# A 512-wide layer in plain float32 instead of three products of high and low fp32r parts

## The reference

```python
# layer 0
h = relu(x)
h = depthwise 3x3 conv of h, dilation 2, + dw_bias
h = h @ pw + pw_bias                      # 256 -> 256
x = h * inv + (beta - moving_mean * inv)  # inv = gamma * rsqrt(moving_var + eps)
# layer 1: a scan over all 56*56 positions on a spiral from the centre outwards
def step(g, (ci, ni, nm, nc)):
    local = g[:, ci, :]
    neigh = (g[:, ni, :] * nm).sum(axis=1) / nc      # up to 4 neighbours
    u = concatenate([local, neigh])                  # 512
    y = tanh(u @ w1 + b1) @ w2 + b2                  # 512 -> 512 -> 1
    g[:, ci, :] = local + y * w_y
```

## Time and profile before

| | |
|---|---|
| median of 3 runs | 5248.01 us (5244.97 to 5255.16) |
| span of the profiled execution | 5242.1 us |
| TensorE / its weight loads busy | 4812.6 us (92%) / 4082.9 us (78%) |
| VectorE busy | 4437.0 us (85%) |
| ScalarE / GpSimd busy | 2045.2 us (39%) / 1133.7 us (22%) |
| mean granted TensorE clock | 0.973 of full speed |
| HBM traffic | 128 GB/s over the span |

### The profile page before, as it was taken

How to read it: one execution, slowest core, us unless ns; L and a number is a source line. 1 busy time by engine, 2 the same in 40 slices (tenths; PEclk the granted TensorE clock), 3 DMA queues, 4 the chain that set the end, 5 groups by cost and what they waited for, 6 DMA issues and landing times.

```text
span 5242.1 us, 101723 instructions
## 1 busy us (share of the span) xinstructions
PE 4812.6 (92%) x26981; PEld 4082.9 (78%) x26981; DVE 4437.0 (85%) x7868; ACT 2045.2 (39%) x3253; POOL 1133.7 (22%) x1806
## 2 busy tenths in 40 slices
PE   4888888988888887999999999999999999999998
PEld 3777777887777776888888877788877887888776
DVE  6999999999999994777777877778777887888888
ACT  3555555555555552333333333333333333333332
POOL 1000000000000000333333333333333333333332
PEclk8999999999999998999999999999999999999999
DMA  4454544544444443433334333333333333333332
GB/s 104 159 164 153 163 154 155 169 163 154 152 159 148 156 151 150 118 114 112 115 109 114 116 111 111 109 110 115 108 105 104 112 109 104 107 112 104 106 100 72
DMA packets 253378, 661.81 MB, mean 126 GB/s; under 512 B 82210, under 2 KB 83234, under 8 KB 238370
## 3 DMA queue, kind: packets, MB, share of 16 engines
q1 hardware_dynamic: 209778, 552.76, 34.6%
q0 software_dynamic: 43056, 102.88, 6.1%
HBM read 347.00 MB, written 323.09 MB: 128 GB/s over the span
## 4 chain that ended last, share of the span: by engine, by line
PE 53%; issue 28%; DVE 17%; DVEq 1%; DMA 1%; SPq 0%; ACT 0%; POOL 0%; ACTq 0%; POOLq 0%
PE psum L785 13%; PE psum L783 13%; PE psum L784 13%; DVE dw_rows L568 9%; PE psum L771 6%; PE psum L779 3%; DVE bias_tmp L617 2%; DVE u_lo L602 2%; PE psum L744 2%; PE psum L750 2%; DVE relu_rows L638 1%; DVE gn_out L625 1%; DVE gn_out L610 0%; DVE win_tmp L643 0%; PE psum L728 0%
## 5 line engine op out<-in xcount | busy, mean ns | idle before, releaser
L568 DVE SCALAR_TENSOR_TENSOR dw_rows<-relu_rows,taps,dw_rows 128x896 f32<-128x896 f32 x1744 | 1863.0, 1145 | 104.0 <-ACT dw_rows L416 46.6
L783 PE MATMUL psum<-w_hi,u_hi 128*128 128x512 f32 x3588 | 1583.8, 441 | 0.0
L785 PE MATMUL psum<-w_hi,u_lo 128*128 128x512 f32 x3588 | 1413.6, 394 | 0.0
L468 ACT ACTIVATE gn_out<-gn_out 128x512 f32<-128x512 f32 x897 | 567.1, 632 | 2147.6 <-DVE gn_out L610 1840.4
L784 PE MATMUL psum<-w_lo,u_hi 128*128 128x512 f32 x3588 | 1401.5, 391 | 0.0
L377 POOL DMA_INDIRECT out<-gn_out,idx_col x897 | 881.9, 983 | 2034.7 <-POOLq L383 1375.4
L610 DVE SCALAR_TENSOR_TENSOR gn_out<-v_row,s_col,psum 128x512 f32<-128x512 f32 x897 | 668.7, 746 | 456.3 <-PE psum L785 387.0
L744 PE MATMUL psum<-pw,dw_rows 128*128 128x256 f32 x3136 | 846.1, 394 | 0.0
L750 PE MATMUL psum<-ident,dw_rows 128*128 128x128 f32 x6216 | 836.5, 279 | 0.0
L750 PEld LDWEIGHTS psum<-ident,dw_rows 128*128 128x128 f32 x6216 | 757.7, 145 | 87.2 <-issue 8.2
L785 PEld LDWEIGHTS psum<-w_hi,u_lo 128*128 128x128 f32 x3588 | 676.5, 189 | 155.4
(11 more groups left out here) (75 smaller groups left out, 2728.3 us busy)
## 6 DMA issues: line engine op xcount, KB each, us to landing
gn_out<-scratch SPq DMA_DIRECT2D x3588, 64.0 KB
scratch<-gn_out SPq DMA_DIRECT2D x112, 1792.0 KB, 5.7
x_tok<-x SPq DMA_DIRECT2D x112, 896.0 KB, 6.6
out<-gn_out,idx_col POOLq DMA_INDIRECT x897
relu_rows<-coef SPq DMA_DIRECT2D x1, 5830.5 KB
gn_out<-L_conv_w SPq DMA_DIRECT2D x2, 512.0 KB, 7.6
store_idx<-store_row SPq DMA_DIRECT2D x1, 448.5 KB, 7.7
w_row<-L_conv_w SPq DMA_DIRECT2D x1, 256.0 KB, 6.0
```

Of the source, the lines that this page charges most:

```text
L468: act.activation(th[:, cc % 2, :], pre_s[:, cc % 2, :], ACT.Tanh).then_inc(th_ready, 1)
L568: ins = dve.scalar_tensor_tensor(out=dst, in0=src, scalar=w, in1=dst, op0=ALU.mult, op1=ALU.add)
L783: pe.matmul(bank, hi, w1_hi[:, k, :], start=False, stop=False)
L785: last = pe.matmul(bank, lo, w1_hi[:, k, :], start=False, stop=k == 2 * CK - 1)
```

## The change

The high and low parts go. `w1_sb` holds the folded w1 and `u_sb` the transposed u, both float32, and `hidden` has one matmul per block of 128 instead of three. `low_part` on VectorE is gone with its semaphore; ScalarE's copy (now `copy_u`) counts up `u_copied`, which TensorE waits for in both places. The four starting credits are given by ScalarE. In the setup four subtractions on VectorE go.

```diff
-        w1_hi = sb("w1_hi", [P, 2 * CK, HID], f32r)
-        w1_lo = sb("w1_lo", [P, 2 * CK, HID], f32r)
-        u_hi = sb("u_hi", [P, U_SLOTS, 2 * C], f32r)
-        u_lo = sb("u_lo", [P, U_SLOTS, 2 * C], f32r)
+        w1_sb = sb("w1_sb", [P, 2 * CK, HID])
+        u_sb = sb("u_sb", [P, U_SLOTS, 2 * C])
...
+            act.sem_inc(u_copied, 4)
...
-            def high_part(c, cc):
+            def copy_u(c, cc):
                 act.wait_ge(u_ready, c + 1)
                 act.wait_ge(pre_ready, c + 1)
-                act.activation(u_hi[:, cc % U_SLOTS, :], psum[:, cc % 4, :], ACT.Copy).then_inc(hi_ready, 1)
+                act.activation(u_sb[:, cc % U_SLOTS, :], psum[:, cc % 4, :], ACT.Copy).then_inc(u_copied, 1)
...
-                link(dve.tensor_copy(w1_hi[:, k, :], w))
-                link(dve.tensor_tensor(w1_lo[:, k, :], w, w1_hi[:, k, :].bitcast(f32), ALU.subtract))
+                link(dve.tensor_copy(w1_sb[:, k, :], w))
...
-            def low_part(c, cc):
-
-                dve.wait_ge(hi_ready, c + 1)
-                slot = cc % U_SLOTS
-                dve.tensor_tensor(u_lo[:, slot, :], psum[:, cc % 4, :], u_hi[:, slot, :].bitcast(f32),
-                                  ALU.subtract).then_inc(lo_ready, 1)
...
-                if not isinstance(c, int) or c + AHEAD < TILES:
-                    low_part(c + AHEAD, cc + AHEAD)
...
-                pe.wait_ge(lo_ready, c + 1)
+                pe.wait_ge(u_copied, c + 1)
...
-                pe.wait_ge(lo_ready, 4 + c + 1)
+                pe.wait_ge(u_copied, 4 + c + 1)
                 pe.wait_ge(pres_ready, c + 1)
                 bank = psum[:, 4 + cc % 4, :]
                 pe.matmul(bank, pick[:, :], bias_rows[:, C:C + HID], start=True, stop=False)
                 for k in range(2 * CK):
-                    hi = u_hi[:, cc % U_SLOTS, P * k:P * (k + 1)]
-                    lo = u_lo[:, cc % U_SLOTS, P * k:P * (k + 1)]
-                    pe.matmul(bank, hi, w1_hi[:, k, :], start=False, stop=False)
-                    pe.matmul(bank, hi, w1_lo[:, k, :], start=False, stop=False)
-                    last = pe.matmul(bank, lo, w1_hi[:, k, :], start=False, stop=k == 2 * CK - 1)
+                    last = pe.matmul(bank, u_sb[:, cc % U_SLOTS, P * k:P * (k + 1)], w1_sb[:, k, :],
+                                     start=False, stop=k == 2 * CK - 1)
                 last.then_inc(pre_ready, 1)
```

More of the change, by code:

```diff
@@ L126, in build @@
           load_row, store_row, coef, wrap, side, scratch, out):
-    f32, f32r = mybir.dt.float32, mybir.dt.float32r
+    f32 = mybir.dt.float32
     bf16, i32 = mybir.dt.bfloat16, mybir.dt.int32
@@ L226, in build @@
         u_ready = sem("u_ready")
-        hi_ready = sem("hi_ready")
-        lo_ready = sem("lo_ready")
+        u_copied = sem("u_copied")
         pre_ready = sem("pre_ready")
@@ L456, in _ @@
             row_steps(act, step, ROWS - 1 + OUT_LAG)
-            def high_part(c, cc):
+            def copy_u(c, cc):
                 act.wait_ge(u_ready, c + 1)
                 act.wait_ge(pre_ready, c + 1)
-                act.activation(u_hi[:, cc % U_SLOTS, :], psum[:, cc % 4, :], ACT.Copy).then_inc(hi_ready, 1)
+                act.activation(u_sb[:, cc % U_SLOTS, :], psum[:, cc % 4, :], ACT.Copy).then_inc(u_copied, 1)
             def tile(c, cc, *_):
                 if not isinstance(c, int) or c + AHEAD < TILES:
-                    high_part(c + AHEAD, cc + AHEAD)
+                    copy_u(c + AHEAD, cc + AHEAD)
                 act.wait_ge(pres_ready, 4 + c + 1)
@@ L470, in _ @@
             for c in range(AHEAD):
-                high_part(c, c)
+                copy_u(c, c)
             tile(0, 0)
@@ L541, in _ @@
             dve.sem_inc(s_ready, 1)
-            dve.sem_inc(lo_ready, 4)
             dve.sem_inc(out_ready, TILE_SLOTS)
@@ L661, in y_of @@
                 return y_lvl[:, level % 2, g:g + 1]
-            for c in range(AHEAD):
-                low_part(c, c)
             centre_y = y_of(1, 0)
             add_s(0, 0, 0, 0)
-            low_part(AHEAD, AHEAD)
             dot(0, 0, centre_y)
@@ L802 @@
 SETUP_T = SETUP_CST + 4
-SETUP_V = SETUP_T + 4 * CK + 1 + 2 + (1 + 6) + (1 + 3) + 1
+SETUP_V = SETUP_T + 2 * CK + 1 + 2 + (1 + 6) + (1 + 3) + 1
 CONV_TAPS = [(1, 0), (1, 2)] + [(ky, kx) for ky in (0, 2) for kx in range(3)]
```

## The result

The changed kernel takes 5765.8 us in the median of 4 runs (5762.2 to 5767.6), the kernel before 5247.4 us. The ratio is 1.098 (95% interval 1.097 to 1.100): 518 us slower. The profiled execution took 5765.57 us, with a span of 5763.8 us.

What follows compares the result with a forecast made beforehand. TensorE was taken to set the second phase's pace, 3.40 us a tile. Span 5242.1 + 512.4 (products) + 20 (jumps) - 2.9 (setup) = 5771.6 us, plus 5.9 around the span: 5777 us, range 5745 to 5825.

Steps and rivals of the forecast that it cites:

- Products: Second phase: twelve fp32r matmuls become eight float32 records of 0.4286 us; tile 3.40 to 4.08 us, +512.4 us.
- Subtraction: VectorE loses 0.683 us per tile, 612 us in all: worth nothing as work; ScalarE's copy gets about 6.5 us to spare.
- Jumps and wrap levels: Second phase's loop jumps: most of 96.9 us excess swallowed, 20 us of TensorE's own idle time stays; bounds 0 and 70.
- Last stage: Last 32 tiles, one per level: VectorE's chain shrinks from 3.98 to 3.78 us, so TensorE's 4.08 us sets the pace.
- ScalarE: Its copy of u writes float32 instead of fp32r, still 0.58 us, its wait stays hidden: no change in time.
- Setup: Before the first phase, four VectorE subtractions of 0.69 us go, about 0.72 us each with the gap: -2.9 us.
- First phase: The phase before the changed lines is untouched: 0 us.
- Around the span: The median of the runs lies 5.9 us over the profiled span (5248.0 against 5242.1), so 5.9 us was added.
- stalls stay: Rival: at loop jumps 6.5 us to spare is not enough, or TensorE idles 3 us; up to 70 us, 5827; chance 0.12.
- every pass costs as much as an fp32r product: Rival: each of a float32 record's two passes takes 0.229 us, 0.236 us more a tile, 5988 us; chance 0.04.
- the late copy: Rival: ScalarE's copy of u comes late every time, tile longer than 4.08 us, some 5900 us; chance 0.02.
- faster: Rival: a float32 record starts every 0.229 us, TensorE's tile 2.48 us, VectorE's chain binds some stages; about 4435 us; chance 0.02.

Runs made afterwards that it cites:

- the bf16 rows: The kernel before with its high and low parts in bf16 instead of fp32r, same twelve products: 5150.5 us, ratio 0.982.
- two versions with pieces: The changed kernel with each 512-column float32 matmul cut into two pieces (8 matmuls a tile) or three (12): 5803.0 us and 5855.3 us.
- the run with two products: The changed kernel with two fp32r products per block (u by w1's high and low parts) instead of one float32 product: 4568.0 us, ratio 0.870.

## Why the prediction was right, point by point

- *Products.* Right, and the whole result hangs on it. A record starts every 0.43 us, a tile takes 4.085 us against my 4.08. From the first to the last tile it is 518.6 us more (3661.9 - 3143.3), where I had 512.4 + 20; 4.5 us of that is the third digit of the pace (3660.2 against 3655.7). The Trainium skill has four passes for true FP32 (FP8 and Floating Point Precision, TensorE Precision Notes). The trace agrees in the time, 0.857 us for a block of two records, or 0.214 us for each of four passes; it has no row for a pass. Where its page "TensorE: Matmul & The Clock Gate" (Back-to-back issue gap) gives N/2.4 + 2.5 ns for a warm matmul, 215.8 ns at 512 columns, the bf16 rows have 217 and the fp32r rows 229. The estimate from the page alone, 5940 us, missed by 174 us, 142 of them (12 x 0.0132 x 896) because it gave an fp32r product 215.8 ns where the rows have 229.
- *Subtraction.* Right: worth nothing as work (5760 us with it), worth 37 us at the new pace through the wait (5797 us with it). The spare time came out at 6.7 us for the 6.5 forecast.
- *Jumps and wrap levels.* This is the term that was mis-sized. I left 20 us for TensorE's own idle time, and it is 0; what is left over the pace is 1.8 us of lower clock in the first interval. The working took the idle time of a program with twelve matmuls a tile, 2.7 us a jump, to a program with four. The runs with eight and twelve matmuls a tile have 10.6 and 18.0 us. The reading of the 97 us before was incomplete too: beside VectorE's jumps and the last stage, some 17 us of it are TensorE's lower clock beside its long pauses, which went with them.
- *Last stage.* Right: 4.08 us between levels, and VectorE waits 0.3 to 0.45 us for TensorE in each. Its own chain is thus about 3.65 us, some 0.1 us shorter than I had it.
- *ScalarE.* Right: 0.58 us as before, never waited for in the second phase.
- *Setup.* Right: 2.94 us for 2.9.
- *First phase.* I had 0. From its first transposes to the first bias matmul of the second phase it took 2033.7 us (2089.3 - 55.66) against 2025.6 us (2084.2 - 58.60), 8 us more. It has no line of the change in it. It need not be variation between executions, though. From the first transposes of the first phase to the first of the second, the traces have 2027.3 us in the changed kernel and 2025.7 and 2026.6 in its two versions with pieces, which have the same program but for the products. The kernel before and all other versions, the two with the subtraction kept among them, have 2014.0 to 2020.6. Why is open.
- *Around the span.* I added 5.9 us, the distance of a median to the span of another execution. The profiled execution of the changed kernel has 1.8 us around its span (5765.57 - 5763.8). 4 us of my error lie there.

In sum: 5242.1 + 518.6 - 2.9 + 8.1 - 2.0 (the last tile to the end, 12.6 against 14.6 us) = 5763.9 us of span, measured 5763.8. The forecast of 5777 us was 11 us high: -14 from pace and jumps together, +8 from the first phase, -2 from the end, -4 from around the span. That the first phase hid a part of the rest is luck.

Of the rivals, "stalls stay" fails with TensorE 99.9% busy, "every pass costs as much as an fp32r product" with 0.43 us a record, the late copy with 6.7 us to spare. For "faster", a float32 record would have had to start every 0.34 us or less; the run with two products shows what such a pace leads to.

## What to carry to other kernels

A float32 matmul is two records here and costs 0.857 us for 512 columns, and three fp32r products cost 0.687 us: where TensorE sets the pace, plain float32 loses a quarter in the products, and the vector work that it saved was worth only what it did to waits. Before adding or removing a wait, read how long before its use each operand is ready and behind what its producer stands in its queue; a step further ahead is worth something only where that spare time is the one that runs out, and costs time where the loads are the next to be late. A pause of TensorE can cost more than its own length, so read the granted clock behind it. Prices for a forecast can come from a few rows of the setup, if shape, type and granted clock are those of the stream: seven steps of 0.4286 us gave the 0.43 of 7176 records.

## What was not expected of the hardware

An fp32r product of 512 columns costs 0.229 us, a bf16 product 0.217, and half a float32 record 0.214, all at the full clock. At the lower clock the surcharge of fp32r is gone: 256 columns take 0.21 us, which is 256 columns at 1.2 GHz. The cause is open; the weight load of 0.19 us is not it, since float32 records of 256 columns with the same load start 0.216 us apart.

TensorE's idle time of its own at the loops' jumps grows in sum with the number of its instructions in the loop: 0, 10.6 and 18.0 us over the kernel with 4, 8 and 12 matmuls a tile, at nearly the same pace. The longest single one is 3.0 us with 8 and 1.7 with 12.

Beside a pause of TensorE the granted clock can fall: in the kernel before, in eight of twelve cases with pauses of 2.4 to 4.3 us.

Loads from the scratch came at one tile in 2.67 us with two products a tile and with one (between 3000 and 3400 us). What sets that pace is open.
